# The first softmax's exponentials, the attended values and the output projection in f16 halves, and two value products moved ahead of the queries' last tiles

## What is computed

```python
def iterative_inv(mat, n_iter=6):
    K = mat
    V = jnp.swapaxes(K, -1, -2) / denom
    for _ in range(n_iter):
        KV = jnp.matmul(K, V)
        V = jnp.matmul(0.25 * V, 13 * I - jnp.matmul(KV, 15 * I - jnp.matmul(KV, 7 * I - KV)))
    return V
# attention, H = 16 heads of 16 channels, M = 64 landmarks (means of 16 tokens each)
kernel1 = softmax(Q K_l)       # 1024 x 64
kernel2 = softmax(Q_l K_l)     # 64 x 64
kernel3 = softmax(Q_l K)       # 64 x 1024
SV = (kernel1 @ iterative_inv(kernel2)) @ (kernel3 @ V)
out = SV @ w_proj
# feed-forward: eight experts' autoencoder losses choose one expert per sequence
h = relu(x @ Wd1[e] + bd1[e]); recon = h @ Wd2[e] + bd2[e]; idx = argmin(mean((recon - x)**2))
y = x @ W_base + b_base + relu(x @ Wa_down[idx] + ba_down[idx]) @ Wa_up[idx] + ba_up[idx]
# x = x + ln(attention(ln(x)));  x = x + ln(feed_forward(ln(x)))
```

## Time and profile before

| | |
|---|---|
| median of 3 runs | 2277.98 us (2277.91 to 2283.66) |
| profiled execution | 2281.05 us, span 2279.3 us |
| mean granted TensorE clock | 0.964 |
| busy share | PE 89%, DVE 65%, ACT 38%, POOL 31% |
| chain that ended last | PE 62%, DVE 17%, SP's queue 9%, ACT 3% |

### The profile page before, as it was taken

The page is one execution under the profiler, slowest core; times in us unless marked ns, Lnnn a source line. Parts: engine busy times, 40 slices in busy tenths (PEclk is TensorE's granted clock), DMA queues, the critical chain, the costliest instruction groups (busy, mean ns, idle before and its releaser), DMA issues.

```text
span 2279.3 us, 58742 instructions
## 1 busy us (share of the span) xinstructions
PE 2019.9 (89%) x24991; PEld 1307.2 (57%) x24991; DVE 1471.1 (65%) x3319; ACT 864.9 (38%) x1509; POOL 700.9 (31%) x916
## 2 busy tenths in 40 slices
PE   3888989999898998989899898989989898998945
PEld 1554747556474755647465564746657475665724
DVE  3667576766757667675766757576675757767531
ACT  3334344343433443343343434334343443334320
POOL 4153152322315232232523224251331424223051
PEclk9889999999999999999999999999999999999978
DMA  6213141221514222151422215132231513213020
GB/s 152 46 47 76 30 122 39 81 61 30 121 30 116 44 73 61 29 131 30 112 44 71 66 30 131 30 99 52 63 79 30 129 31 89 62 41 83 11 56 19
DMA packets 232972, 150.71 MB, mean 66 GB/s; under 512 B 153035, under 2 KB 203732, under 8 KB 232693
## 3 DMA queue, kind: packets, MB, share of 16 engines
q1 hardware_dynamic: 232710, 146.95, 27.5%
HBM read 36.98 MB, written 16.78 MB: 24 GB/s over the span
## 4 chain that ended last, share of the span: by engine, by line
PE 62%; DVE 17%; SPq 9%; issue 4%; ACT 3%; POOL 3%; DMA 2%; DVEq 1%; POOLq 0%; ACTq 0%
PE NS L979 11%; PE ringF L1187 9%; SPq L429 9%; PE ringF L1172 6%; PE KV L1060 5%; PE ringA L1146 5%; PE ringA L880 5%; PE ringF L1220 3%; PE ringA L1046 3%; PE ringA L1022 3%; DVE stage L1608 3%; DVE mx L1518 2%; PE ringF L880 2%; PE ringF L1222 2%; ACT E L690 2%
## 5 line engine op out<-in xcount | busy, mean ns | idle before, releaser
L1187 PE MATMUL ringF<-x,H 128*128 128x256 f16 x1536 | 237.9, 273 | 0.0
L1532 DVE TENSOR_REDUCE mx<-ringA 128x8 f32<-128x512 f32 x256 | 175.4, 685 | 89.3 <-PE ringA L1022 88.8
L682 ACT ACTIVATE E<-ringA,score_scale 128x512 f32<-128x512 f32 x256 | 175.5, 686 | 116.8 <-PE ringA L1046 116.7
L1187 PE MATMUL ringF<-H 128*128 128x128 f16 x1024 | 204.4, 220 | 1.4 <-DVE H L1619 1.4
L880 PE MATMUL ringA<-xT,wqkv 128*128 128x512 f16 x768 | 184.0, 391 | 21.2 <-ACT QS L700 11.7
L1585 DVE SCALAR_TENSOR_TENSOR X<-X,NS 128x320 f32<-128x320 f32 x160 | 78.0, 488 | 182.8 <-PE NS L979 177.7
L1518 DVE TENSOR_REDUCE mx<-ringA 128x1 f32<-128x512 f32 x256 | 160.1, 682 | 52.0 <-PE ringA L1013 51.5
L1172 PE MATMUL ringF<-wd,x2T 128*128 128x512 f16 x768 | 187.9, 384 | 6.4 <-DVE H L1619 3.1
L516 POOL TENSOR_SCALAR vtmp<-mv,eps_ffn 128x8 f32<-128x8 f32 x16 | 5.1, 316 | 612.0 <-DVE mv L1363 612.0
L690 ACT ACTIVATE E<-ringA,score_scale 128x512 f32<-128x512 f32 x256 | 158.6, 684 | 75.2 <-PE ringA L1077 75.2
L516 POOL TENSOR_SCALAR vtmp<-mv,eps_ln 128x8 f32<-128x8 f32 x32 | 9.9, 310 | 538.2 <-DVE mv L1363 538.2
(11 more groups left out here) (261 smaller groups left out, 4317.8 us busy)
## 6 DMA issues: line engine op xcount, KB each, us to landing
KS<-stage SPq DMA_DIRECT2D x384, 64.0 KB, 2.0
QS<-stage SPq DMA_DIRECT2D x384, 64.0 KB, 2.0
xin<-in_L_attn_x_dram SPq DMA_DIRECT2D x16, 1024.0 KB, 11.0
xres<-in_L_attn_x_dram SPq DMA_DIRECT2D x16, 1024.0 KB, 8.1
out_dram<-yout SPq DMA_DIRECT2D x16, 1024.0 KB, 5.5
QS<-LB SPq DMA_DIRECT2D x16, 512.0 KB, 4.4
E<-in_L_attn_w_qkv_dram SPq DMA_DIRECT2D x1, 768.0 KB, 7.0
H<-in_L_ffn_Wd_dram SPq DMA_DIRECT2D x2, 256.0 KB
```

The costliest lines, as they stand in the source:

```text
L682: A(E[:, k % ESLOTS, :], ps[:, :], ACT.Exp, scale=score_scale[:, 0:1]).then_inc(freed["s3"].sem, 1)
L1187: ins = MM(dst, H[:, a, t, own], src, start=first and i == 0, stop=last and i >= 3, skip_group_check=True)
L1532: V_.reduce_max(mx1[:, t, 8 * h:8 * h + 8], take(b, "m1", k)[:, :].rearrange("p (a m) -> p a m", a=8), AX.X)\
```

## The change

What it does:
- `exp1` writes an f16 exponential (E1, in the memory of E, high half) and the same exponential again in f32 (E1f, two slots). A subtraction E1f - high gives the low half: for the first twelve (`LOWS`) on POOL, between `norm1(b+1)` and `ffn_residual(b-1)` (in batch 0 ahead of `ffn_weights`), for the last four on DVE. `exp1` k waits for the low half of k-2.
- `sum_exponentials` makes two f16 passes with `sel16`, `attend` three with Yblk in halves. Both wait for the low halves where they waited for the exponentials.
- Yblk, scaled by 0.25, is made in three steps on DVE: f32 result, high half, low half.
- The attended values are computed in f32 in the memory of `xtmp` (xsv), ACT copies the high half to `stage` (`attended_hi`), DVE subtracts the low one (`attended_lo`), and the output projection runs in three f16 passes with `wproj` in halves. POOL makes these in `ffn_weights`, three steps more.
- The order `output_projection` (0, 1), `attend` 3 becomes projection 0, `attend` 3, projection 1.
- `values` 2 and 3 and the tiles `pk` 6 and 7: the maxima 0 to 7 come with `values` 2 and 3 between them, ahead of `pk` 6; `pk` 7 follows the maxima 8 and 9. On ACT the copies of `values` 2 and 3 now stand ahead of `halves2` and of the last tiles' high halves.

```diff
@@ USES_A
-                  + [("m3", k) for k in range(4)] + [("pk", 6), ("m3", 4), ("pk", 7)]
...
+                  + [("m3", k) for k in range(4)] + [("pv", 2)] + [("m3", k) for k in range(4, 8)] + [("pv", 3), ("pk", 6)]
+                  + [("m3", 8), ("m3", 9), ("pk", 7)] + [("m3", k) for k in range(10, 16)] + [("f3", 0)])
@@ POOL
+            def exponentials1_lo(b):
+                for k in range(LOWS):
+                    pool.wait_ge(freed["s1"].sem, freed["s1"].at(b, k + 1))
+                    pool.sem_inc(s_apart, 1)
+                    pool.tensor_tensor(E1[:, k % ESLOTS, 1, :], E1f[:, k % 2, :], E1[:, k % ESLOTS, 0, :], ALU.subtract).then_inc(e1_lo.sem, 1)
...
                 if more:
                     norm1(b + 1)
+                exponentials1_lo(b)
                 if first(b):
                     ffn_weights()
@@ ACT, exp1(b, k)
-                A(E[:, k % ESLOTS, :], ps[:, :], ACT.Exp, scale=score_scale[:, 0:1]).then_inc(freed["s1"].sem, 1)
+                if k >= LOWS + 2:
+                    act.wait_ge(e1_lo2.sem, e1_lo2.at(b, k - LOWS - 1))
+                elif k >= 2:
+                    act.wait_ge(e1_lo.sem, e1_lo.at(b, k - 1))
...
+                A(E1[:, k % ESLOTS, 0, :], ps[:, :], ACT.Exp, scale=score_scale[:, 0:1])
+                A(E1f[:, k % 2, :], ps[:, :], ACT.Exp, scale=score_scale[:, 0:1]).then_inc(freed["s1"].sem, 1)
+            def attended_hi(b, i):
+                act.wait_ge(freed["sv"].sem, freed["sv"].at(b, i + 1))
+                A(stage[:, i % 2, 0, (i // 2) * HALF:(i // 2 + 1) * HALF], xsv[:, i % 2, :], ACT.Copy).then_inc(sv_hi.sem, 1)
@@ ACT, body
                 staged(b, (2,))
+                values(b, (2, 3))
                 if ffn:
                     halves2(b - 1, (0,))
                 staged(b, (3,))
                 if ffn:
                     halves2(b - 1, (1,))
-                values(b, (2, 3))
@@ PE
-                pe.wait_ge(freed["s1"].sem, freed["s1"].at(b, GP * (i + 1)))
+                if i < LOWS // GP:
+                    pe.wait_ge(e1_lo.sem, e1_lo.at(b, GP * (i + 1)))
+                else:
+                    pe.wait_ge(e1_lo2.sem, e1_lo2.at(b, GP * (i + 1) - LOWS))
...
-                        pe.wait_ge(freed["sv"].sem, freed["sv"].at(b, 2 + k))
+                        pe.wait_ge(sv_lo.sem, sv_lo.at(b, 2 + k))
...
-                        for kc in range(KC):
-                            ins = MM(ps[:, i * C:(i + 1) * C], svT[:, kc, t * P:(t + 1) * P], wproj[:, kc, :],
-                                     start=kc == 0, stop=kc == KC - 1)
+                        ins = three(ps[:, i * C:(i + 1) * C], lambda a, kc: stage[:, kc, a, t * P:(t + 1) * P],
+                                    lambda a, kc: wproj[:, a, kc, :])
@@ DVE, body
-                for i in range(2):
-                    attended(b, i)
-                for part in range(2):
-                    invert_sums(b, 2, part)
+                attended(b, 0)
+                attended(b, 1)
+                attended_lo(b, 0)
+                attended_lo(b, 1)
+                exponentials1_lo(b, 12)
+                invert_sums(b, 2, 0, more)
+                exponentials1_lo(b, 13)
+                invert_sums(b, 2, 1, more)
+                exponentials1_lo(b, 14)
+                exponentials1_lo(b, 15)
                 attended(b, 2)
-                for part in range(2):
-                    invert_sums(b, 3, part)
+                invert_sums(b, 3, 0, more)
+                attended_lo(b, 2)
+                invert_sums(b, 3, 1, more)
                 attended(b, 3)
+                attended_lo(b, 3)
```

161 lines of the change are left out of this document (104 added, 57 removed).

## The result

The changed kernel takes 2483.84 us (median; 2479.69 to 2484.8), the kernel before 2277.94 on the same chip: 1.0906 times, 95% interval 1.0882 to 1.093. The direction was right and the size was not: 2408 was forecast, with a range that ended at 2460. The profiled execution's span is 2482.0 us against 2279.3, and the mean granted clock 0.916 of full speed against 0.964.

A forecast was written before the change was run, and what follows sets the result against it. PE was busy 89%, but at a batch's end PE, ACT and DVE were about level, so added work sets it. 16 x (6.2 + 0.5) + 15 x (0.5 + 0.3) + 11 = 130 more gave 2408 us; range 2345 to 2460.

The forecast's parts named there:

- term (b): End of a batch: POOL's feed-forward residual lies under DVE's new subtractions; 0 to +2.3 us, +0.5 taken, 16 times.
- (a): Inverse iterations: DVE's operation G meets POOL's low halves of 1.15 us; 0 to +1.5 a batch, +0.5 taken, 15 batches.
- rival 2: PE's clock falls to half speed in the end of a batch too: +3 us a batch, 2456 us; chance 0.15.
- The walk through the end of a batch: Last stretch priced step by step across ACT, POOL, DVE and PE: next batch starts 6.2 us later, bounds +3 and +9.
- Its first step: End of a batch: ACT's exponentials take 1.2 us each, with two copies between, ending at 967.9 instead of 962.6.
- Order: Values before the queries' last tiles: maxima 2 us earlier, next stage no earlier; +0.3 us a batch, bounds -2 and +1.
- Batch 0: Once: POOL's later, longer weight preparation delays its attention residual, and DVE waits behind it; +11 us, bounds 5 and 13.
- Rival 3: End of a batch: ACT and DVE hide their new work, PE's shorter products decide; -3.2 us a batch, 2238; chance 0.04.

The follow-up runs named there:

- the projection alone: Changed kernel with f32 exponentials: only attended values and projection in f16 halves, plus the new order; 2398.11 us, or 2330.93 with POOL's two residual adds cut to 8 elements.
- order-alone kernel: Kernel before the change with only the value products and the queries' last tiles in the new order; 2285.94 us, ratio 1.0045.

## Why the prediction was wrong

By its own steps:

- **Port, term (b): the step that failed, and (a) with it.** "POOL's residual lies under DVE's new subtractions: 0 to +2.3, I take +0.5." With the adds cut the end is 2.4 us shorter (27.56 to 25.13), and with the projection alone 4.1. Of the 2.4, 1.5 are the last subtraction standing for the second add, and 1.0 the half clock that went with it. Together with (a) the standing makes 30 of the 73 us that the forecast lacks. I took a value near the lower end, although the one row that showed such a meeting (1.78) spoke for the upper one. I also priced a stall by one add of 2.34. That fits the changed kernel, but in others a subtraction stood through both (3.66, 4.33, 4.80). The Trainium skill, SBUF — State Buffer, section "SBUF: two separate sides", says that whoever starts first has the shared ports for the whole instruction and the other fully blocks. The traces agree: the waiting instruction ended some 0.55 us after the other's end. In part of the meetings they go further, and the loser waited for the next instructions of the run as well.
- **The clock: a term that the sum had at nothing.** It stood as rival 2 (+3 us a batch, chance 0.15) and not in the forecast. The clock fell in the end of a batch as that rival said, and the projection's second half, which rival 2 named, took 3.76 us on the mean instead of 2.79: 1.0 a batch. The fourth sum took 1.04 instead of 0.62 as well, and DVE waits for it; filling the hole before it gave those 0.4 back, but the last subtraction lost them again at POOL's add. No run takes the clock away alone, so what it would cost without the adds is open.
- **The walk through the end of a batch (6.2 of it).** Right in its places and nearly in its times: PE waited at the three points named, the third sum came 7.8 us after the first product as worked out, and the last product was done after 20.2 us where 19.1 was worked out. With the adds out of the way the end is 7.4 longer than before, so 1.2 of the walk is missing, and that was not taken apart. Its first step, ACT's pace, was not what decides: with the adds cut, cutting ACT's work changed nothing (end 25.13 both times), cutting DVE's changed 2.3. The plan named both and added them in one chain.
- **Port, term (a): mis-sized.** 0.5 taken, 1.7 measured, where +1.5 was the upper bound. Two of the five G a batch meet a low half, not one (1.40 together), and a copy waits too (0.35).
- **Order: mis-sized.** 0.3 taken, 0.75 here and about 10 us over the kernel when alone. The copies ran at 995.92 and 1000.23 in the order-alone kernel (995.9 and 1000.0 were worked out), so the mechanism was right; moving them cured it.
- **Batch 0.** 11 forecast, 11.9 measured, by the wait that was named.
- **The range.** Both port terms at their upper bounds would have given 2408 + 16 x 1.8 + 15 x 1.0 = 2452, inside 2460. The result lies outside because several terms came out high at once: (a) 1.7 for 0.5, (b) 1.5 for 0.5, the clock 1.0 for nothing, the walk 7.4 for 6.2, the order 0.75 for 0.3. Terms (a) and (b) are one cause, and (b) and the clock hang together, so their errors should not have been taken as apart. Rival 2's 2456 was near the result, but by luck: it had +3 a batch for the clock and only 0.5 for each port term.
- **Rival 3** (ACT and DVE hide it) is refuted: PE is idle at all three places.

The difference between forecast and result is 76 us, and 73 between the spans' 202.7 and 130: ends 48, inversions 16.5, the order 7.4 and batch 0 0.9 more than forecast. Of the ends' 48, some 14 are DVE's standing at POOL's adds beyond the 0.5 taken, some 14 the half clock in the projection's second half, and the remaining 20 the walk's (7.4 instead of 6.2 a batch).

## What to carry to other kernels

Before handing POOL or DVE a subtraction or sum of two SBUF tensors, list every such instruction of the other engine that may run then. Price the meeting between the rest of the instruction under way and the whole rest of the other's run, since both happened here, and do it at the instruction that has a chain behind it: here a reciprocal. A stall of that kind depends on where the two meet, so cutting work elsewhere can make a kernel slower (30 us for less work on ACT), and an experiment that only removes work does not tell its price as long as such stalls are there. Take the stalls away first, then compare. And look at batches one by one: the means here hide ends of two or three kinds, and it is their difference that shows the clock.
